# Attention of a seven-layer kernel: from head by head to units of four heads by 512 queries

## The chip, the core and the metric

The kernel runs on one core of a Trainium2 chip. The time is the device's, in microseconds (us), from one execution to the next of the whole program; less is better. The engines are PE (TensorE, with its weight loads PEld), DVE (VectorE), ACT (ScalarE), POOL (GpSimd) and SP (SyncE, which here only issues DMAs).

## The reference

One sequence of 2048 tokens of 128 channels passes through a chain of layers, each added to x: softmax attention with 16 heads of 8 channels (rotary positions, RMS norm of q and k), a small spline feed-forward, retention, the feed-forward again, linear attention, then twice a layer with a convolution, softmax attention and a mixture of four experts, with an RWKV layer between the two. Softmax attention so stands three times in the program, and is all that the change touches:

```python
attn = jnp.einsum('bqhd,bkhd->bhqk', q, k) * scale
attn = jnp.where(causal[None, None], attn, -jnp.inf)
attn = jax.nn.softmax(attn, axis=-1)
out = jnp.einsum('bhqk,bkhd->bqhd', attn, v).reshape(B, T, C)
```

All in float32, with B = 1, T = 2048, C = 128, 16 heads, D = 8.

## The kernel before

`qkv_stage` (L424) projects q, k and v, splits q and k into three bf16 parts each (so that nine products of parts give float32 precision) and stores them, turned, in DRAM as `q_parts` and `k_parts`. After a barrier `attention_stage` (L682) begins, and after it `output_stage` turns and projects the result.

Attention goes head by head. For a head SP loads 72 rows (3 x 3 parts x 8 channels) of q and of k, 2048 columns each, twice: into `q_max`/`k_max` for the maxima and into `q_exp`/`k_exp` for the scores (`load_rows`, L768, L769; six DMAs of 96 KB for each pair of buffers). All four have two slots, for even and odd heads.

The pass over maxima (`max_unit`, PE L902, DVE L1021) puts queries on partitions: a product of 128 queries by up to 512 keys, on the diagonal a second product that adds the mask (L905), and a reduction on DVE, through a ring of three PSUM banks `stat`. A head has 41 such reductions. When a group of query tiles is complete DVE makes its maximum, split into a high and a low bf16 (`row_max`, L1030 to L1032); PE turns these (`shift_unit`, L911), DVE copies them out (L1039), and SP writes them as two more rows below the 72 of `q_exp` (`load_shift`, L797), against rows of -1 in `k_exp`. So the second product gives the score minus its row's maximum. There are three such groups per head.

The second pass puts keys on partitions. A unit is two key tiles by 512 queries, 1024 columns (less on the diagonal); a head has 20 (`EXPU`). PE makes the scores (L924) into one of two double banks, ACT takes the exponential into one of four slots of `probs` (L884), POOL zeroes the triangle on the diagonal (L854), and PE multiplies with the values (`pv`, L934). The values of a head, with a column of ones for the denominator, are 32 columns of weights; the four query tiles of 128 columns go to the four strips of 32 columns of the array, so that eight products of 128 columns serve a unit. They accumulate in one bank for the whole head, which ACT copies out (L873), PE turns (L915) and DVE divides (L1045, L1046).

The order on PE is written out by hand: for each unit e it waits for exponential e, issues the scores of e + 2, the values of e, and the entries of `PLAN` for e, which are the maxima of the next head, spread evenly (two a unit), and at fixed places the shift rows and the output of the head before. The first head's 41 maxima come ahead of everything (`FIRST_PLAN`), and the last head runs without maxima. PE and DVE walk the ring in the same order. Heads 1 to 14 are a loop over pairs of heads on every engine. POOL gathers the values of the next head (L833).

SP's order is, for each head: the loads of maxima for head h + 2, those of scores for h + 1, then the shift rows.

Of the kernel before, what the change touches and what calls it, by code (L numbers as in the profile page):

```python
# [89 lines left out]
def load_stage(k, d, w):  # L90

    nc = k.nc
    with ExitStack() as ctx:
# [15 lines left out]
        with nc.Block() as block:  # L109
# [22 lines left out]
            @block.vector  # L132
            def _(dve):
                for n, name in enumerate(("q_max", "q_exp")):
                    nc.vector.memset(w[name][64:P, :, :], 0.0).then_inc(padded[0].sem, 1)
                dve.wait_ge(loaded.sem, loaded.at(16 * len(plain)))
                nc.vector.tensor_copy(w["mask16"][:], maskf[:]).then_inc(kept.sem, 1)
                nc.vector.tensor_copy(w["ident16"][:], w["ident"][:]).then_inc(kept.sem, 1)

            @block.gpsimd  # L140
            def _(pool):
                for n, name in enumerate(("k_max", "k_exp")):
                    nc.gpsimd.memset(w[name][64:P, :, :], -1.0).then_inc(padded[1].sem, 1)
                    pool.wait_ge(padded[1].sem, padded[1].at(n + 1))

        loaded.done(16 * len(plain))
        for sig in padded:
            sig.done(2)
# [532 lines left out]

def attention_stage(k, w, v, parts_dram, scale, y):  # L682

    nc = k.nc
    MAXU = []
    for i in range(NT):
        pieces = [(c * BANK, min(BANK, (i + 1) * P - c * BANK)) for c in range(i // QC + 1)]
        if i == NT - 1:
            pieces[0:1] = [(0, BANK // 2), (BANK // 2, BANK // 2)]
        MAXU += [(i, at, width, n) for n, (at, width) in enumerate(pieces)]
    EXPU = []  # L700
    for j in range(NQ):
        for u in range(2 * j):
            EXPU.append((j, [(2 * u, 0), (2 * u + 1, 0)]))
        EXPU.append((j, [(QC * j, 0), (QC * j + 1, 1)]))
        EXPU.append((j, [(QC * j + 2, 2), (QC * j + 3, 3)]))
    NM, NE = len(MAXU), len(EXPU)

    OWN = [e for e in range(NE) if EXPU[e][1][0][0] >= QC * EXPU[e][0]]
    VT = NT // len(OWN)
    VN = len(OWN) - 1  # L710
    GROUPS = [(0, 2), (2, 3), (3, 4)]
    NG = len(GROUPS)
    MAX_END = [sum(i < QC * hi for i, *_ in MAXU) for _, hi in GROUPS]
    FIRST_EXP = [min(e for e in range(NE) if EXPU[e][0] == lo) for lo, _ in GROUPS]


    OWN_AT, NEXT_AT, OUT_AT = 2, (9, 15), 0
    PLAN = []
    for e in range(NE):
        if e == OWN_AT:  # L720
            PLAN.append((e, "own_shift", NG - 1))
        for g, at in enumerate(NEXT_AT):
            if e == at:
                PLAN.append((e, "next_shift", g))
        PLAN += [(e, "max", u) for u in range(e * NM // NE, (e + 1) * NM // NE)]
        if e == OUT_AT:
            PLAN.append((e, "out", None))
    HEAD0_PLAN = [p for p in PLAN if p[1] != "out"]
    LAST_PLAN = [p for p in PLAN if p[1] in ("own_shift", "out")] + [(NE, "own_out", None)]
    FIRST_PLAN = [(0, "max", u) for u in range(NM)] + [(0, "next_shift", g) for g in range(NG - 1)]  # L730
    STATU, PRE = len(PLAN), len(FIRST_PLAN)
    AT, AT0 = ({(kind, arg): n for n, (_, kind, arg) in enumerate(plan)} for plan in (PLAN, HEAD0_PLAN))
    for g, at in enumerate(NEXT_AT):
        assert AT["max", MAX_END[g] - 1] < AT["next_shift", g]
    RING, PSLOTS = 3, 4
    assert STATU % RING == 0 and NE % PSLOTS == 0 and NE % 2 == 0
    TAIL = PRE - 1 + (H - 1) * STATU
    counts = []
    with ExitStack() as ctx:
        qm, km, qe, ke = w["q_max"], w["k_max"], w["q_exp"], w["k_exp"]  # L740
        probs = k.sb("probs", [P, PSLOTS, 2 * BANK], F32, ctx)
        vh = k.sb("v_head", [P, 2, NT, 32], F32, ctx)
        early = k.sb("v_early", [P, 2 * VT, D], F32, ctx)
        mpart = k.sb("max_part", [P, 2, NT, NQ + 1], F32, ctx)
        mx = k.sb("row_max", [P, 2, NT], F32, ctx)
        mxb = k.sb("row_max_parts", [P, 2, SHIFT * NT], BF16, ctx)
        mxt = [k.sb(f"row_max_turned{g}", [SHIFT * QC * (hi - lo), 2, P], BF16, ctx) for g, (lo, hi) in enumerate(GROUPS)]
        ot = k.sb("out_turned", [P, 2, BANK], F32, ctx)
        rden = k.sb("inv_denominator", [P, 2, NT], F32, ctx)
        ring = [k.ps(f"stat{n}", [P, BANK], ctx) for n in range(RING)]  # L750
        sc = [k.ps(f"score{n}", [P, 2 * BANK], ctx) for n in range(2)]
        acc = k.ps("pv", [P, BANK], ctx)

        m_loaded = [k.counter(f"max_rows_loaded{n}") for n in range(2)]
        e_loaded = [k.counter(f"exp_rows_loaded{n}") for n in range(2)]
        shift_in = [[k.counter(f"shift_rows_loaded{n}_{g}") for g in range(NG)] for n in range(2)]
# [3 lines left out]
        out_copied, v_ready, cut = k.counter("pv_copied_out"), k.counter("v_head_ready"), k.counter("probs_masked")  # L760
        v_early = k.counter("v_early_rows")
        q_rows, k_rows = (parts_dram[s].rearrange("a (h d) t -> h a d t", d=D) for s in range(2))

        def load_rows(sp, qt, kt, par, h, loaded):

            for a in range(PARTS):
                at = slice(a * PARTS * D, (a + 1) * PARTS * D)
                sp.dma_start(qt[at, par, :], bcast(q_rows[h, a], 0, PARTS)).then_inc(loaded.sem, 16)  # L768
                sp.dma_start(kt[at, par, :], k_rows[h]).then_inc(loaded.sem, 16)  # L769

        NL = 2 * PARTS * 16
        NS = SHIFT * 16

        def base(h):

            return PRE if isinstance(h, int) and h == 0 else h * STATU + (PRE - 1)

        with nc.Block() as block:


            @block.sync
            def _(sp):
                def load_max(h, par):
                    load_rows(sp, qm, km, par, h, m_loaded[par])

                def load_exp(h, par, prev):
                    if prev is not None:
                        sp.wait_ge(scored.sem, scored.at(NE * prev + NE))
                    load_rows(sp, qe, ke, par, h, e_loaded[par])

                def load_shift(par, g, used):
                    sp.wait_ge(stat_used.sem, stat_used.at(used))
                    lo, hi = GROUPS[g]
                    nt = QC * (hi - lo)
                    for n in range(SHIFT):
                        r = KROWS + n
                        sp.dma_start(qe[r:r + 1, par, lo * BANK:hi * BANK].rearrange("o (i q) -> o i q", q=P),  # L797
                                     mxt[g][n * nt:(n + 1) * nt, par, :]).then_inc(shift_in[par][g].sem, 16)
# [4 lines left out]
                for g in range(NG - 1):  # L803
                    load_shift(0, g, NM + g + 1)
# [1429 lines left out]
```

## Time and profile before

| what | time |
|---|---|
| median of three runs | 3068.51 us |
| lowest and highest | 3059.32 and 3070.42 us |
| span of the profiled execution | 3064.6 us |
| PE busy | 2459.5 us (80%) |
| DVE busy | 1968.9 us (64%) |
| ACT busy | 1467.3 us (48%) |
| POOL busy | 542.6 us (18%) |

The profile gives no time of its own for the profiled execution beside its span; the median of the runs is 3.9 us above the span. Busy times are sums over the whole program. As PE is pipelined and the ends of its products are modelled, its busy share is no measure of how near it is to its peak: distances between starts say more. The clock that the chip grants PE is at one of two levels, 1.2 or 2.4 GHz; in a stretch the profile gives the mean as a share of the higher.

### The profile page before, as it was taken

Reading aid. Unit: us, or ns where it says so; the run is one execution under the profiler, and the core shown is the slowest. Engines: PE = TensorE matmul, PEld = TensorE weight load, DVE = VectorE, ACT = ScalarE, POOL = GpSimd, SP = SyncE. Lnnn points to the kernel's source line nnn. Section 1 sums busy time; section 2 is a strip of 40 time slices with the busy share of each in tenths; the row PEclk is TensorE's granted clock in tenths of the full one; section 3 lists DMA queues with packets and bytes.
Section 4 is the critical chain, followed back from the end, with each engine's and each line's share of the span. In section 5 each row is a group of like instructions: output and inputs, shape, how many; then the busy total and the mean of one; then the engine's idle time right before and its main releaser. Section 6 shows DMA issues by size and latency. Waiting matters only on the chain. (4 is left out here: it accounts for less than half of the span.)

```text
span 3064.6 us, 68154 instructions
## 1 busy us (share of the span) xinstructions
PE 2459.5 (80%) x23684; PEld 1331.0 (43%) x23684; DVE 1968.9 (64%) x4246; ACT 1467.3 (48%) x2102; POOL 542.6 (18%) x1023
## 2 busy tenths in 40 slices
PE   3698998994699538648998999897138899999898
PEld 2244444453344325424444444565123444444565
DVE  6576676757477774567777776334957677777333
ACT  3254455564599545334555555323233555555422
POOL 4011111111244315140111111000340111111100
PEclk7699999996799768869999999999668999999899
DMA  3101110000111000010010000000011000010000
GB/s 105 71 33 37 38 38 34 33 10 0 57 48 49 12 0 1 0 65 32 33 40 36 31 31 24 1 0 0 0 50 44 35 31 31 38 40 23 1 1 14
DMA packets 45622, 89.65 MB, mean 29 GB/s; under 512 B 9104, under 2 KB 27792, under 8 KB 45456
## 3 DMA queue, kind: packets, MB, share of 16 engines
q1 hardware_dynamic: 45456, 87.34, 7.8%
q8 instruction: 116, 1.90, 0.3%
q14 instruction: 50, 0.41, 0.0%
HBM read 73.29 MB, written 13.63 MB: 28 GB/s over the span
## 5 line engine op out<-in xcount | busy, mean ns | idle before, releaser
L1021 DVE TENSOR_REDUCE max_part<-stat 128x1 f32<-128x512 f32 (+3 forms) x1968 | 1074.9, 595 | 407.8 <-PE stat L902 203.0
L884 ACT ACTIVATE probs<-score 128x1024 f32<-128x1024 f32 (+1 forms) x960 | 859.5, 896 | 807.0 <-PE score L924 804.7
L934 PE MATMUL pv<-probs,v_head 128*32 128x128 f32 x13056 | 635.4, 285 | 0.5 <-POOL probs L854 0.5
L924 PE MATMUL score<-q_exp,k_exp 128*128 128x512 bf16 (+3 forms) x1920 | 536.5, 363 | 121.0 <-DMA q_exp<-row_max_turned 100.0
L902 PE MATMUL stat<-k_max,q_max 128*128 128x512 bf16 (+3 forms) x1968 | 581.7, 365 | 64.0 <-DMA k_max<-k_parts 48.4
L934 PEld LDWEIGHTS pv<-probs,v_head 128*32 128x32 f32 x13056 | 367.7, 111 | 301.7 <-issue 279.8
L902 PEld LDWEIGHTS stat<-k_max,q_max 128*128 128x128 bf16 x1968 | 162.0, 100 | 324.2 <-DVE max_part L1021 131.5
L833 POOL COPY v_head<-qkv 128x16 f32 (+2 forms) x258 | 51.1, 199 | 1191.1 <-ACT probs L884 1190.4
L924 PEld LDWEIGHTS score<-q_exp,k_exp 128*128 128x128 bf16 x1920 | 140.9, 98 | 276.3 <-issue 209.4
L1978 ACT ACTIVATE gate<-gate_ps 128x512 f32<-128x512 f32 x128 | 76.4, 597 | 264.0 <-PE gate_ps L1953 264.0
L854 POOL TENSOR_SCALAR_AFFINE_SELECT probs<-probs 128x256 f32<-128x256 f32 x384 | 155.9, 406 | 251.4 <-ACT probs L884 251.2
L1652 ACT ACTIVATE abs_act_ps<-abs_act_ps 128x1024 f32<-128x1024 f32 (+3 forms) x176 | 167.5, 952 | 27.4 <-PE abs_act_ps L1607 27.3
L905 PE MATMUL stat<-mask,ident 128*128 128x128 bf16 x768 | 174.9, 230 | 0.0
L2018 DVE TENSOR_TENSOR hidden<-value_ps,gate 128x512 f32<-128x512 f32 x128 | 88.6, 692 | 112.1 <-PE value_ps L1954 112.0
L1684 DVE TENSOR_REDUCE abs_part<-abs_dve_ps 128x512 f32 (+5 forms) x224 | 108.5, 515 | 44.4 <-PE abs_dve_ps L1621 43.2
L1953 PE MATMUL gate_ps<-ln_t,expert_wv 128*128 (+1 forms) x256 | 133.2, 602 | 0.0
L1954 PE MATMUL value_ps<-ln_t,expert_wv 128*128 (+1 forms) x256 | 132.5, 599 | 0.0
L1943 PEld LDWEIGHTS expert_ps<-expert_proj,hidden 128*128 128x128 f32 x1024 | 119.2, 192 | 17.7 <-issue 17.7
L1943 PE MATMUL expert_ps<-expert_proj,hidden 128*128 128x128 f32 x1024 | 119.6, 275 | 1.8 <-DVE hidden L2018 1.8
L905 PEld LDWEIGHTS stat<-mask,ident 128*128 128x128 bf16 x768 | 79.7, 104 | 65.8 <-issue 12.5
L1607 PE MATMUL abs_act_ps<-k_max,q_max 128*128 128x512 bf16 x352 | 100.0, 371 | 7.0 <-ACT abs_act_ps L1652 4.2
L2007 DVE SCALAR_TENSOR_TENSOR X<-expert_ps,pick,X 128x128 f32 (+1 forms) x128 | 37.5, 346 | 98.2 <-PE expert_ps L1943 98.2
(268 smaller groups left out, 2569.8 us busy)
## 6 DMA issues: line engine op xcount, KB each, us to landing
q_max<-q_parts SPq DMA_DIRECT2D x192, 96.0 KB
k_max<-k_parts SPq DMA_DIRECT2D x192, 96.0 KB
q_exp<-q_parts SPq DMA_DIRECT2D x144, 96.0 KB
k_exp<-k_parts SPq DMA_DIRECT2D x144, 96.0 KB
q_parts<-parts_t SPq DMA_DIRECT2D x16, 384.0 KB, 2.6
k_parts<-parts_t SPq DMA_DIRECT2D x16, 384.0 KB, 3.3
q_exp<-row_max_turned SPq DMA_DIRECT2D x192, 1.0 KB
expert_wv<-in_L_ffn_expert_wv SPq DMA_DIRECT2D x1, 2048.0 KB, 8.5
```

Of the source, the lines that this page charges most:

```text
L854: nc.gpsimd.affine_select(tile, tile, [[0, 2], [1, P]], ALU.is_ge, 0.0, base=0, channel_multiplier=-1).then_inc(cut.sem, 1)
L884: nc.scalar.activation(probs[:, e % PSLOTS, 0:width], sc[e % 2][:, 0:width], ACT.Exp, scale=scale).then_inc(expd.sem, 1)
L902: last = nc.tensor.matmul(out[:, 0:width], qm[:, par, i * P:(i + 1) * P], km[:, par, at:at + width], start=True, stop=not own)
L905: last = nc.tensor.matmul(out[:, width - P:width], w["ident16"][:], w["mask16"][:], start=False, stop=True)
L924: last = nc.tensor.matmul(out, ke[:, par, kt * P:(kt + 1) * P], qe[:, par, j * BANK + f * P:(j + 1) * BANK], start=True, stop=True)
L934: last = nc.tensor.matmul(acc[32 * c:32 * c + 32, j * P:(j + 1) * P], vh[:, par, kt, :], probs[:, e % PSLOTS, at:at + P], start=kt == 0, s ...
L1021: nc.vector.reduce_max(mpart[:, par, i, col:col + 1], ring[at % RING][:, 0:width], AX.X).then_inc(stat_used.sem, 1)
L1652: nc.scalar.activation(ps, ps, ACT.Abs, accum_out=part[:, bass.ds(h, 1), i, 0:1]).then_inc(a_used.sem, 1)
L1684: nc.vector.tensor_reduce(part[:, bass.ds(h, 1), i, slot:slot + 1], d_ps[n % DRING][:, 0:width], AX.X, ALU.add, apply_absolute_value=True) ...
L1943: ins = nc.tensor.matmul(op[e % 2][:, s * P:(s + 1) * P], hid[:, e % 2, f, s * P:(s + 1) * P], w["expert_proj"][:, e % E, f, :], start=f = ...
L1953: nc.tensor.matmul(gp[g % 2][:], w["expert_wv"][:, e, f * P:(f + 1) * P], rhs, start=True, stop=True).then_inc(upped.sem, 1)
L1954: nc.tensor.matmul(vp[g % 2][:], w["expert_wv"][:, e, DFF + f * P:DFF + (f + 1) * P], rhs, start=True, stop=True).then_inc(upped.sem, 1)
```

## The change

A unit is now four heads by 512 queries, against all keys up to them: 16 units, in the order `UNITS` (group of heads, block j of queries), each of 4(j + 1) steps of one key tile, 160 steps in all. A step has two score products of 512 columns for each half of the heads, one exponential for each half, and four value products of 512 columns, one per head, each with nine columns of weights (8 channels and the ones) in a strip of its own. `attention_plan` makes the order of the ring: maxima of later units, spread so that each unit's are complete some three steps before its first step, shift rows once per unit (after the first three maxima of the next one), outputs three steps after a unit's end. The ring has 640 maxima, 16 shift rows and 16 outputs. Both passes share one set of rows, in three buffers (`uq`, `uk`); a unit's rows come by 24 DMAs, twelve of 24 KB for the queries and twelve of 24(j + 1) KB for the keys, and the rows of -1 by 12 DMAs at the start. The values are copied once into `v9`. Everything is unrolled, with no loop. `probs` has six slots of half a step. `q_exp` and `k_exp` are gone from the weights, with their memsets in `load_stage`, and `qkv_stage` is called ahead of `softmax_layer`, whose result goes over q's place in `qkv`. The core of the diff, where "..." stands for what is left out:

```diff
+HG = 4
+NG = H // HG
+BUFS = 3
+UNITS = [(0, 0), (0, 1), (0, 2), (0, 3), (1, 3), (2, 3), (3, 3), (1, 2), (2, 2), (3, 2), (1, 1), (1, 0), (2, 1), (2, 0), (3, 1), (3, 0)]
+def attention_plan():
+    steps = [(u, kt) for u, (_, j) in enumerate(UNITS) for kt in range(QC * (j + 1))]
+    first = [min(t for t, (v, _) in enumerate(steps) if v == u) for u in range(len(UNITS))]
+    last = [max(t for t, (v, _) in enumerate(steps) if v == u) for u in range(len(UNITS))]
+    stream, due = [], []
+    for u, (_, j) in enumerate(UNITS):
+        maxima = [("max", u, (h, s, c)) for s in range(QC) for c in range(j + 1) for h in range(HG)]
+        stream += maxima[:LATE] if u else maxima
+        if u:
+            stream.append(("shift", u - 1, None))
+            stream += maxima[LATE:]
+        due.append((len(stream) + LATE + 1, max(1, first[u] - 3) if u else 0))
+    stream.append(("shift", len(UNITS) - 1, None))
+    free = [min(first[u - BUFS + 1] + 3, first[u - 1] - 2) if u >= BUFS else -1 for u in range(len(UNITS))]
+    ring, at = [], 0
+    for t in range(-1, len(steps)):
+        for half in range(2):
+            for u in range(len(UNITS)):
+                if t == last[u] + 3 and half == 1:
+                    ring.append((t, half, "out", u, None))
+            if t < 0:
+                want = due[0][0] if half else 0
+            else:
+                room = [(min(n, len(stream)) - at, 2 * (d - t) - half) for n, d in due]
+                want = at + max([0] + [-(-n // max(1, left)) for n, left in room if n > 0])
+            while at < min(want, len(stream)) and t >= free[stream[at][1]]:
+                ring.append((t, half) + stream[at])
+                at += 1
...
+LATE = 3
...
+                def load(u):
+                    g, j = UNITS[u]
+                    b = u % BUFS
+                    if u >= BUFS:
+                        sp.wait_ge(scored.sem, scored.at(2 * LAST[u - BUFS] + 2))
+                    keys = BANK * (j + 1)
+                    for h in range(HG):
+                        for a in range(PARTS):
+                            at = slice(a * PARTS * D, (a + 1) * PARTS * D)
+                            sp.dma_start(uk[at, b, h, 0:keys], k_rows[g * HG + h][:, :, 0:keys]).then_inc(loaded[b].sem, 16)
+                            sp.dma_start(uq[at, b, h, :], bcast(q_rows[g * HG + h, a][:, j * BANK:(j + 1) * BANK], 0, PARTS)).then_inc(loaded[b].sem, 16)
...
+                load(0)
+                sp.wait_ge(minus_ready.sem, minus_ready.at(1))
+                for b in range(BUFS):
+                    for h in range(HG):
+                        sp.dma_start(uk[KROWS:ROWS, b, h, :].rearrange("r (c t) -> r c t", t=BANK), bcast(minus[:], 1, NQ)).then_inc(minus_loaded.sem, 16)
+                load(1)
+                load(2)
+                load_shift(0)
+                for u in range(NU):
+                    if u + 1 < NU:
+                        load_shift(u + 1)
+                    if u + BUFS < NU:
+                        load(u + BUFS)
...
+                        if kind == "max" and arg == (0, 0, 0):
+                            pe.wait_ge(loaded[u % BUFS].sem, loaded[u % BUFS].at(loads_of(u)))
+                        elif kind == "shift":
+                            pe.wait_ge(max_ready.sem, max_ready.at(u + 1))
+                        elif kind == "out":
+                            pe.wait_ge(out_copied.sem, out_copied.at(u + 1))
...
+                def pv(t):
...
+                    for h in range(HG):
+                        last = nc.tensor.matmul(acc[32 * h:32 * h + D + 1, f:BANK], v9[:, kt, g * HG + h, :], probs[:, (2 * t + h // 2) % PSLOTS, h % 2, 0:BANK - f],
+                                                start=kt == 0, stop=kt == QC * j + QC - 1, tile_position=(0, 32 * h))
...
+                for t in range(NS):
+                    pe.wait_ge(expd.sem, expd.at(2 * t + 1))
+                    if t + 1 < NS:
+                        scores(t + 1, 0)
+                    fill_ring(t, 0)
+                    if t > 0:
+                        pv(t - 1)
+                    pe.wait_ge(expd.sem, expd.at(2 * t + 2))
+                    if t + 1 < NS:
+                        scores(t + 1, 1)
+                    fill_ring(t, 1)
...
-                for n, name in enumerate(("k_max", "k_exp")):
-                    nc.gpsimd.memset(w[name][64:P, :, :], -1.0).then_inc(padded[1].sem, 1)
+                nc.gpsimd.memset(w["k_max"][64:P, :, :], -1.0).then_inc(padded[1].sem, 1)
```

## Rows read from the trace of the kernel before

**Rows 1.** Stretches, first to last exponential of each stage: length, each engine's busy time, granted clock, DMA.

```profile
127.30:674.90 547.60, 499.19 (x5932) 247.12 (x5929) 376.14 (x826) 294.87 (x335) 69.27 (x253) 0.94 0.09 34
1391.30:1926.10 534.80, 496.27 (x5931) 244.18 (x5929) 375.27 (x826) 294.52 (x335) 68.60 (x253) 0.95 0.09 33
2325.30:2858.90 533.60, 494.14 (x5931) 243.66 (x5929) 375.33 (x826) 294.55 (x335) 68.59 (x253) 0.96 0.09 33
```

**Rows 2.** Instructions of line 884 by stage: ns min/median/max, first and last start.

```profile
L884 ACT ACTIVATE probs<-score x320: 484/1024/1026, 127.3 to 674.4; 128x1024 f32<-128x1024 f32 x96, 128x896 f32<-128x896 f32 x64
L884 ACT ACTIVATE probs<-score x320: 484/1024/1026, 1391.3 to 1925.6; 128x1024 f32<-128x1024 f32 x96, 128x896 f32<-128x896 f32 x64
L884 ACT ACTIVATE probs<-score x320: 484/1024/1026, 2325.3 to 2858.4; 128x1024 f32<-128x1024 f32 x96, 128x896 f32<-128x896 f32 x64
```

**Rows 3.** Waits, 1400 to 1900 us: in total, times, longest.

```profile
PE score L924 <- DMA q_exp<-row_max_turned: 34.8, 14, 3.2
```

**Rows 4.** Timeline, second stage: a unit of a head with maxima (start, length, engine).

```profile
1434.34 0.61 PE L924 MATMUL score<-q_exp,k_exp 128*128 128x512 bf16 x2
...
1434.88 0.65 PE L934 MATMUL pv<-probs,v_head 128*32 128x128 f32 x16
...
1435.46 0.60 PE L902 MATMUL stat<-k_max,q_max 128*128 128x512 bf16 x2
...
1435.90 0.59 PE L924 MATMUL score<-q_exp,k_exp 128*128 128x512 bf16 x2
```

**Rows 5.** Timeline, second stage: units of the last head, without maxima.

```profile
1921.94 0.60 PE L924 MATMUL score<-q_exp,k_exp 128*128 128x512 bf16 x2
...
1922.48 0.64 PE L934 MATMUL pv<-probs,v_head 128*32 128x128 f32 x16
...
1923.06 0.61 PE L924 MATMUL score<-q_exp,k_exp 128*128 128x512 bf16 x2
```

**Rows 6.** Stretches of 0.02 us, value products alone: PE records under way in brackets.

```profile
311.36:311.38 0.02, 0.02 (x4) 0.02 (x4) 0.00 (x0) 1.00 0.53 205
...
311.48:311.50 0.02, 0.02 (x6) 0.02 (x7) 0.00 (x0) 1.00 0.00 0
```

**Rows 7.** Groups by line: busy us, mean ns, idle before; experts' gate products and value products.

```profile
L1953 PE MATMUL gate_ps<-ln_t,expert_wv 128*128 (+1 forms) x256 | 133.2, 602 | 0.0
L934 PE MATMUL pv<-probs,v_head 128*32 128x128 f32 x4332 | 210.3, 285 | 0.0
```

**Rows 8.** Timeline, start of the first attention stage.

```profile
89.51 0.91 SPq L768 DMA_DIRECT2D q_max<-q_parts  x1
...
98.72 0.70 SPq L768 DMA_DIRECT2D q_exp<-q_parts  x1
99.46 0.70 SPq L769 DMA_DIRECT2D k_exp<-k_parts  x1
...
100.71 5.89 DVE L1021 TENSOR_REDUCE max_part<-stat 128x1 f32<-128x128 f32 x12 [10.90 <-PE stat L905]
...
123.81 2.65 SPq L797 DMA_DIRECT2D q_exp<-row_max_turned  x4
...
126.40 1.23 PE L924 MATMUL score<-q_exp,k_exp 128*128 128x512 bf16 x4 [3.58 <-DMA q_exp<-row_max_turned]
```

**Rows 9.** Stretches of 1 us, stores and loads; last two columns: DMA share of 16 engines, GB/s.

```profile
87.00:88.00 1.00, 0.00 (x0) 0.00 (x0) 0.00 (x0) 0.00 (x0) 0.00 (x0) 0.50 0.99 355
97.00:98.00 1.00, 0.00 (x0) 0.00 (x0) 0.00 (x0) 0.00 (x0) 0.00 (x0) 0.50 0.18 74
```

**Rows 10.** SP's instructions by line, whole program: ns min/median/max; shift rows, then stores.

```profile
L797 SPq DMA_DIRECT2D q_exp<-row_max_turned x288: 572/614/742, 123.8 to 2844.2; - x144
L655 SPq DMA_DIRECT2D q_parts<-parts_t x16: 372/372/407, 64.1 to 2283.1; - x16
L655 SPq DMA_DIRECT2D k_parts<-parts_t x16: 477/489/1402, 64.6 to 2283.6; - x16
```

More of the change, by code:

```diff
@@ L676, in qkv_stage @@
                 sig.done(NQ)
+HG = 4
[30 more added lines that the diff above has]
+                at += 1
+    for u in range(len(UNITS)):
+        if last[u] + 3 >= len(steps):
+            ring.append((len(steps), 1, "out", u, None))
+    assert at == len(stream)
+    return steps, first, last, ring
@@ L706, in attention_stage @@
[L706 to L734, printed above, removed]
@@ L918, in scores @@
-                def scores(e, par):
-                    j, tiles = EXPU[e]
-                    at = 0
-                    for kt, f in tiles:
-                        width = BANK - f * P
-                        out = sc[e % 2][:, at:at + width]
-                        last = nc.tensor.matmul(out, ke[:, par, kt * P:(kt + 1) * P],
-                                                qe[:, par, j * BANK + f * P:(j + 1) * BANK], start=True, stop=True)
-                        at += width
-                    last.then_inc(scored.sem, 1)
@@ new lines, in scores @@
+                def scores(t, hp):
+                    u, kt = STEPS[t]
+                    b, f = u % BUFS, first_col(t)
+                    if hp == 0 and t == FIRST[u]:
+                        pe.wait_ge(shift_in.sem, shift_in.at(SHIFT * 16 * (u + 1)))
+                    for i in range(2):
+                        h = 2 * hp + i
+                        last = nc.tensor.matmul(sc[hp][:, i, 0:BANK - f], uk[0:ROWS, b, h, kt * P:(kt + 1) * P], uq[0:ROWS, b, h, f:BANK],
+                                                start=True, stop=True)
+                    last.then_inc(scored.sem, 1)
@@ L1073, in _ @@
-                body(0, None, 0, plan=HEAD0_PLAN)
-                before = steps[1]
-                body(1, None, 1)
-                per_head = steps[1] - before
-                before = steps[1]
-                with dve.Fori(1, H // 2 - 1) as i:
-                    for par in range(2):
-                        steps[0], steps[1] = i * (2 * per_head) + (before - 2 * per_head), par * per_head
-                        body(2 * i + par, i, par)
-                steps[0], steps[1] = before + (H - 4) * per_head, 0
```

476 lines of the change are left out of this document (175 added, 301 removed).

## The prediction

> **What bounds the kernel now.** I began with the stretches between the first and the last exponential of the three attention stages [rows 1]. They last 547.6, 534.8 and 533.6 us, over half of the span of 3064.6 us. PE is busy for 91 to 93% of each, DVE 69 to 70%, ACT 54 to 55%, POOL 13%, and the clock granted is 0.94 to 0.96, nearly all at the 2.4 GHz level. So PE's order of work sets the pace there, and I looked for what PE spends beside streaming. The first and last times of the exponentials [rows 2] with the timeline of a stage's start [rows 8] give what lies ahead: from SP's first load at 89.5 to the first exponential at 127.3, 37.8 us; the other stages issue the same loads in the same order, and I take the same. The waits of one stage [rows 3] show PE's only large one: 34.8 us in 14 waits for a head's shift rows. Two pieces of the timeline give the step. With maxima, scores begin at 1434.34, value products at 1434.88, maxima at 1435.46, the next scores at 1435.90: 1.56 us [rows 4]. In the last head, without maxima, scores begin every 1.12 us (1921.94, 1923.06) [rows 5]. An exponential of 1024 columns takes 1.02 us [rows 2].
>
> **What the step is made of.** Two maxima cost PE 0.44 us, 0.22 per 512 columns of bf16 [rows 4], so two score products stream 0.43 too. The 16 records of the value product start four at a time, about 0.11 to 0.12 us apart [rows 6], so they stream some 0.43. The step of 1.12 thus holds 0.86 of streaming and 0.26 of changing over: scores to values takes 0.54 for 0.43, values to the next 0.58 for 0.43 [rows 4, 5].
>
> **The value products.** The same columns stream: four heads by 512 columns in four column strips instead of four query tiles of one head. A record of 512 fp32 columns lasts 602 ns and one of 128 columns 285 [rows 7]: 384 more columns cost 0.32, so 512 stream 0.43, and the two records of a product 0.85, the streaming of two old units. What falls away is one change-over in two: 0.26 for each of 160 steps. A full step without ring work costs PE 2 x 0.43 + 0.85 + 0.26 = 1.97, below ACT's 2 x 1.02 + gaps = 2.15. With four ring entries it is 1.97 + 0.88 + about 0.05 for masks = 2.9, where before two units took 3.12. Exponentials keep their number, 320, and their columns.
>
> That four strips stream abreast is seen here at 128 columns [rows 6]; at 512 columns nothing here shows it, and I take it over from there. A page speaks against this: in the Trainium skill (TensorE: Matmul & The Clock Gate, Part 3, the table of measured speedups) packing four tiles of 512 columns gained 3.07 times, not four. By that figure the step's 0.85 would be 1.11, an estimate from the page; the rows at 128 columns do not agree with it.
>
> **Start of a stage, +28 us.** Ahead of the first shift rows SP will issue 24 loads for unit 0, 12 for the -1 rows, and 24 each for units 1 and 2: 84, where it issued 18. Issues of this pattern begin 0.74 apart [rows 8]. Landing does not bind: three of the sixteen engines carry them (share 0.18) at 74 GB/s [rows 9], and the new ones carry 24 to 96 KB, mostly in rows of 1 to 3 KB. Stores in rows of 1 KB moved 355 GB/s at a share of 0.99, 22 per engine [rows 9]; three engines do 66, so 24 KB takes 0.37. Only a pair of 96 + 24 KB (j = 3) needs 120/74 = 1.62 against 1.48, some 19.5 a load. Then 84 x 0.743 = 62.4; from the shift issue to the scores 2.59, to the exponential 0.94 [rows 2, 8]: 65.9 against 37.8. Unit 0 needs only 16 maxima where head 0 needed 41, but they wait for nothing that ends last any more. Clearing the accumulator, the ones and the copy of v (POOL, ACT, DVE) lie under these 66 us; with that cover gone the copy of 2048 columns would cost about 2 us.
>
> **The body.** The plan written in the diff, counted out: step 0 gets 33 ring entries, steps 1 to 18 six each, 19 to 112 four, and in the last 47 steps 13 get six to eight, 5 four, 8 two or three, 21 none or one. DVE back to back took 5.89 us for 12 reductions of 384 columns on average, 0.49 each [rows 8].
> - Step 0: 33 x 0.53 = 17.5 (a mean of 406 columns, and the small operations).
> - Steps 1 to 18: 448 columns, 6 x 0.56 = 3.4; 61.
> - Steps 19 to 112: 94 x 2.9 = 273, less 10: in 28 diagonal steps the shorter scores and values gain until DVE's 4 x 0.6 = 2.4 binds; 263.
> - The last 47: 13 x 3.3 + 5 x 2.9 + 8 x 2.3 + 10 x 2.15 + 11 x 1.5 (diagonal) = 114.
> - 16 turned outputs at 0.8 and 16 ends of maxima, when the ring waits for three small operations, at 0.6: 23.
>
> Together 478. Then the wait that the change adds. SP may load unit u+3 only when unit u has all its scores; 24 issues take 17.8 us and the last lands some 1.9 later, 19.7. PE waits for it at that unit's first maximum, and scores, values and shift rows of the earlier units are queued behind it. The plan sets what lies between. For unit 12 the load may begin half way in step 122 and the maximum stands in step 127: half a step 0.7, a diagonal one 1.2, three without ring work at 2.25, together 8.7, so PE lacks 11. In the same way unit 11 (steps 110 to 115, 11.0 us) lacks 9, unit 13 (130 to 134, 8.9) 11, unit 14 (134 to 139, 14.4, its load held up 2 by shift rows) 7, unit 15 (142 to 146, 8.8) 11, units 9 and 10 (6 steps, 16.5) 3 each, unit 3 2: 57, and 3 more for shift rows behind a load on SP. That is 60, in the place of 34.8 of shift waits. Sum 538, against 547.6, 534.8 and 533.6: -10, +3, +4. Out of the loop's registers the code runs unrolled; I cost fetching it at nothing, since PE needs fewer instructions than before per step.
>
> The memsets that load_stage loses lie under its input loads, and the move of qkv_stage out of softmax_layer only changes lifetimes: nothing.
>
> **Sum.** 3 x 28 - 3 = +81 to +82: 3064.6 + 82 = 3146.6 for the span. The median of the runs, 3068.5, is 3.9 above the profiled span: **3150 us**, 2.7% slower.
>
> Bounds. An issue costs between 0.47 (0.37 and 0.49 of the stores, with the gap of 0.04) and 0.95 (0.91 of a stage's first load) [rows 8, 10]. I take 0.74, from the same pattern. The late waits lie between 0 and 90 us a stage, the full step between 2.7 and 3.1 (+-19 us a stage).
>
> **Rivals.**
> A, not slower: with their short rows the new loads issue faster. Shift rows, of 256 bytes, issue in 0.57 to 0.74, median 0.61 [rows 10], 0.65 with the gap: the start gains 8, seven late waits 2.2 each, 23 a stage, giving 3081. At 0.47 the start gains 23, the waits 41: 2958. It decides from about 0.61 per issue down. For: the size of the rows is all that changes. Against: the stores have rows of 1 KB too, and there every issue moves four times the bytes of a load for 0.4, so size does not seem to set it; the pattern (24 rows on three engines) stays. 0.19.
> B, the late waits hardly appear, because steps there run longer than I put them or a unit's loads land sooner: minus 57 x 3, 2979. Against: SP's issues alone fill 17.8. 0.07.
> C, one strip in four runs alone at 512 columns: 0.85 x 4/3 = 1.14, 0.28 more on 136 full steps' worth, 39 a stage: 3266. For: nothing of that width here. Against: all four abreast at 128 [rows 6]. 0.09. It is the case of the page named above.
> D, the strips don't run abreast at nine columns of weights: 3 x 0.85 x 136 more a stage, near 4190. 0.02.
> E, a row of 1 KB costs an engine as much as one of 4 KB: 1.28 per load; start +45, waits +100 a stage: near 3590. Against: the stores [rows 9]. 0.02.
> The forecast has 0.61, its own range 3085 to 3215.
>
> **How the numbers follow.** About 0.5% is what a measurement tells from no change (3053 to 3084). Faster: the lower half of A, B, a little of the forecast's tail, 0.17. Same: the rest of A and some tail, 0.14. Slower: 0.69. The range reaches into A and B below and to C above and leaves out the rest: 3030 to 3260.
>
> **What would show it.** The first exponential 66 us after SP's first load; SP's issues 0.74 apart; PE waiting for unit loads at the first maximum of units 11 to 15, 7 to 11 us each; a full step of 2.9 with four entries; values of 0.85 + 0.2 as a group of eight records; the wait for shift rows down to some us. If the steps with four entries take over 3.1, the packing step is wrong; if the start takes under 55, the issue price is; if the stage's last third shows no waits for loads, the plan's slack was misread. All three low at once would make it faster than before.

## The result, and the profile after

The changed kernel takes **3179.1 us** (median of 4 runs, 3176.3 to 3187.3), the kernel before 3069.5 in the same session (4 runs): a ratio of 1.037, 95% interval 1.034 to 1.039. I had predicted 3150, 2.7% slower; it is 3.7% slower. The run profiled took 3187.3 with a span of 3185.6, which is 121.0 more than before's 3064.6. It is the slowest of the four, 8 us above their median, so that the accounts below, which go by its profile, hold that much more than the medians do.

From the page of the kernel after: span, busy times, and four groups of the attention stages.

```profile
span 3185.6 us, 41521 instructions
PE 2347.6 (74%) x14293; PEld 1042.1 (33%) x14324; DVE 1873.6 (59%) x3816; ACT 1435.5 (45%) x2105; POOL 486.3 (15%) x635
L944 DVE TENSOR_REDUCE max_part<-stat 128x1 f32<-128x512 f32 (+3 forms) x1920 | 1044.8, 604 | 610.5 <-PE stat L851 339.2
L851 PE MATMUL stat<-unit_k,unit_q 72*128 72x512 bf16 (+3 forms) x1920 | 632.0, 386 | 360.7 <-DMA unit_q<-q_parts 320.5
L892 PE MATMUL score<-unit_q,unit_k 74*128 74x512 bf16 (+3 forms) x1920 | 541.8, 369 | 55.6 <-DMA unit_q<-row_max_turned 50.5
L905 PE MATMUL pv<-probs,v_ones 128*9 128x512 f32 (+3 forms) x3840 | 477.2, 570 | 1.6 <-ACT out_turned L828 0.7
```

No engine is fuller than before. What is new stands in the idle columns: TensorE's maxima (L851) waited 320.5 us for the rows of a unit, 138 of them at the three starts and 183 late in the stages.

Stretches from the first to the last exponential of the three stages (to hold against [rows 1]); below them the second stage cut at the starts of steps 19 and 113.

```profile
153.20:705.30 552.10, 472.92 (x2847) 151.93 (x2844) 356.67 (x710) 282.15 (x335) 51.24 (x128) 0.88 0.08 26
1445.60:1998.70 553.10, 474.91 (x2842) 152.44 (x2843) 356.38 (x709) 282.42 (x335) 51.03 (x127) 0.88 0.08 26
2427.50:2978.60 551.10, 472.24 (x2842) 151.49 (x2844) 356.30 (x709) 282.13 (x335) 51.03 (x127) 0.88 0.08 26
...
1538.00:1817.70 279.70, 267.43 (x1644) 85.50 (x1643) 216.59 (x413) 169.27 (x195) 22.42 (x56) 0.96 0.08 28
1817.70:1998.70 181.00, 122.05 (x800) 40.82 (x801) 65.28 (x153) 78.28 (x102) 22.11 (x55) 0.80 0.07 20
```

TensorE is busy 21 to 26 us less in a stage than before, yet the stretches are 4.5, 18.3 and 17.5 us longer, and the granted clock fell from 0.94 to 0.96 to 0.88.

The start of the second stage, SP's queue and the first scores and exponential (compare [rows 8]):

```profile
1378.92 0.79 SPq L782 DMA_DIRECT2D unit_k<-k_parts  x1
1379.76 0.73 SPq L783 DMA_DIRECT2D unit_q<-q_parts  x1
...
1441.14 1.21 SPq L791 DMA_DIRECT2D unit_q<-row_max_turned  x2
...
1444.57 1.86 PE L892 MATMUL score<-unit_q,unit_k 74*128 74x512 bf16 x4 [17.14 <-DMA unit_q<-row_max_turned]
...
1445.62 2.82 ACT L837 ACTIVATE probs<-score 128x1024 f32<-128x1024 f32 x3 [61.44 <-PE score L892]
```

The loads are issued 0.74 us apart, the shift rows follow 62.2 us after the first load, the first exponential after 66.7 (66.2 and 66.6 in the other stages), where the stage before took 37.8. Three starts of +28.7 are +86, three bodies +40; the rest of the program is 5 shorter: 121.

A full step with four maxima in the same stage (timeline, from the scores of one to those of the next), and TensorE's waits for a unit's rows late in the stage:

```profile
1648.11 1.04 PE L905 MATMUL pv<-probs,v_ones 128*9 128x512 f32 x8
1649.09 0.60 PE L892 MATMUL score<-unit_q,unit_k 74*128 74x512 bf16 x2
...
1651.02 1.04 PE L905 MATMUL pv<-probs,v_ones 128*9 128x512 f32 x8
1651.99 0.61 PE L892 MATMUL score<-unit_q,unit_k 74*128 74x512 bf16 x2
```

```profile
1753.18 1.04 PE L851 MATMUL stat<-unit_k,unit_q 72*128 72x512 bf16 x2 [3.73 <-DMA unit_q<-q_parts]
1794.03 0.61 PE L851 MATMUL stat<-unit_k,unit_q 72*128 72x512 bf16 x1 [2.67 <-DMA unit_q<-q_parts]
1834.07 0.29 PE L851 MATMUL stat<-unit_k,unit_q 72*128 72x128 bf16 x1 [9.72 <-DMA unit_q<-q_parts]
1876.18 1.46 PE L851 MATMUL stat<-unit_k,unit_q 72*128 72x512 bf16 x3 [12.22 <-DMA unit_q<-q_parts]
1912.67 0.29 PE L851 MATMUL stat<-unit_k,unit_q 72*128 72x128 bf16 x1 [11.89 <-DMA unit_q<-q_parts]
1935.78 1.46 PE L851 MATMUL stat<-unit_k,unit_q 72*128 72x512 bf16 x3 [8.17 <-DMA unit_q<-q_parts]
1970.55 0.29 PE L851 MATMUL stat<-unit_k,unit_q 72*128 72x128 bf16 x1 [11.90 <-DMA unit_q<-q_parts]
```

The step lasts 2.90 us, and the values of four heads lead to the next scores after 0.97 to 0.98: the eight products would stream 3.4 us one after another at 0.43 each, so four strips run abreast at 512 columns too. The seven waits are those of units 9 to 15, 60.3 us (61.6 and 60.9 in the other stages); unit 3 has none.

### The profile page after: what moved, and what is told of

It reads as the page before. It is cut to its first block and busy times, and to the rows that moved or that the text cites. A ratio compares the mean times of both kernels' runs of the same rounds, so it can differ in the third digit from the quotient of the medians.

```text
span 3185.6 us, 41521 instructions
## 1 busy us (share of the span) xinstructions
PE 2347.6 (74%) x14293; PEld 1042.1 (33%) x14324; DVE 1873.6 (59%) x3816; ACT 1435.5 (45%) x2105; POOL 486.3 (15%) x635
## 5 line engine op out<-in xcount | busy, mean ns | idle before, releaser
L944 DVE TENSOR_REDUCE max_part<-stat 128x1 f32<-128x512 f32 (+3 forms) x1920 | 1044.8, 604 | 610.5 <-PE stat L851 339.2
L837 ACT ACTIVATE probs<-score 128x1024 f32<-128x1024 f32 x960 | 828.4, 896 | 984.1 <-PE score L892 979.5
L851 PE MATMUL stat<-unit_k,unit_q 72*128 72x512 bf16 (+3 forms) x1920 | 632.0, 386 | 360.7 <-DMA unit_q<-q_parts 320.5
L892 PE MATMUL score<-unit_q,unit_k 74*128 74x512 bf16 (+3 forms) x1920 | 541.8, 369 | 55.6 <-DMA unit_q<-row_max_turned 50.5
L905 PE MATMUL pv<-probs,v_ones 128*9 128x512 f32 (+3 forms) x3840 | 477.2, 570 | 1.6 <-ACT out_turned L828 0.7
L851 PEld LDWEIGHTS stat<-unit_k,unit_q 72*128 72x128 bf16 x1920 | 196.2, 103 | 683.8 <-DMA unit_q<-q_parts 331.0
L892 PEld LDWEIGHTS score<-unit_q,unit_k 74*128 74x128 bf16 x1920 | 142.7, 100 | 524.6 <-ACT probs L837 246.6
L1498 PE MATMUL abs_act_ps<-k_max,q_max 128*128 128x512 bf16 (+1 forms) x321 | 93.6, 371 | 12.9 <-ACT abs_act_ps L1543 8.8
L905 PEld LDWEIGHTS pv<-probs,v_ones 128*9 128x9 f32 x3840 | 58.9, 89 | 124.3 <-issue 103.9
L967 DVE RECIPROCAL inv_denominator<-stat 128x16 f32<-128x16 f32 x48 | 12.4, 258 | 125.9 <-PE stat L863 125.9
```

What stands on the lines that cost most here:

```text
L837: nc.scalar.activation(probs[:, n % PSLOTS, :, 0:width], sc[hp][:, :, 0:width], ACT.Exp, scale=scale).then_inc(expd.sem, 1)
L851: last = nc.tensor.matmul(out[:, 0:width], uq[0:KROWS, b, h, s * P:(s + 1) * P], uk[0:KROWS, b, h, c * BANK:c * BANK + width], start=True, ...
L892: last = nc.tensor.matmul(sc[hp][:, i, 0:BANK - f], uk[0:ROWS, b, h, kt * P:(kt + 1) * P], uq[0:ROWS, b, h, f:BANK], start=True, stop=True)
L905: last = nc.tensor.matmul(acc[32 * h:32 * h + D + 1, f:BANK], v9[:, kt, g * HG + h, :], probs[:, (2 * t + h // 2) % PSLOTS, h % 2, 0:BANK ...
L944: nc.vector.reduce_max(mpart[:, u % 2, col, c:c + 1], ring[n % RBANKS][:, 0:width], AX.X).then_inc(stat_used.sem, 1)
```

## The experiments

The theory to be tested: the time lost is issue time on SP's queue, at the start of a stage and again when a short unit frees its buffer; a part of the body that the prediction did not have hangs on TensorE's clock. The rivals: the landing of small DMAs, VectorE's pace, and the change-over between full-array products and strips.

### Units 9 to 15 load nothing

```
 def load(u):
...
+    if u >= KEEP:      # 9
+        return
```

> Units 9 to 15 load no rows of keys and queries (they compute on what lies in the buffer; their shift rows are still loaded). Left out: 7 x 24 of the 384 load DMAs of a stage. If late loads are what the first maxima of units 9 to 15 wait for, as SP issues 24 DMAs in 17.8 us after the unit three before it has ended: the 60.3 us of these waits in a stage go, and the stage body falls from 552 to about 492-498 us, the program from 3179 to about 3000 (-180). If the time only moves (VectorE or the exponentials bound the short units, or the plan's maxima then wait elsewhere), less than half of it comes back: over 3090. The start of the stages (66 us) and the four-entry step (2.9 us) stay as they are in either case.

Measured: **2959.5 us** (2 runs, 0.966 of before, interval 0.963 to 0.969) with units 9 to 15 computing on old rows, 219.6 less than with the loads, 40 more than the waits account for. The first three lines are steps 0 to 18 of the three stages, the last two the second stage's steps 19 to 112 and 113 to the end:

```profile
154.80:241.50 86.70, 77.89 (x401) 24.07 (x399) 74.16 (x145) 34.69 (x41) 6.50 (x16) 0.86 0.10 35
1363.80:1456.10 92.30, 85.34 (x402) 26.12 (x399) 74.37 (x145) 34.71 (x40) 6.50 (x16) 0.76 0.09 33
2267.40:2365.10 97.70, 91.41 (x402) 27.55 (x399) 74.72 (x145) 34.74 (x40) 6.50 (x16) 0.70 0.09 31
...
1456.10:1720.00 263.90, 257.81 (x1643) 84.10 (x1643) 215.80 (x412) 168.80 (x194) 22.42 (x56) 1.00 0.06 21
1720.00:1836.30 116.30, 107.92 (x797) 37.23 (x794) 65.09 (x154) 78.02 (x102) 22.09 (x55) 1.00 0.01 1
```

Two things follow. With the waits, the clock's falls behind them go as well. The same 800 products of the last 47 steps keep TensorE busy for 107.9 us at a clock of 1.00, and for 122.1 at 0.80 in the changed kernel; steps 19 to 112 for 257.8 at 1.00 against 267.4 at 0.96. In the changed kernel's trace the clock falls to 1.2 GHz in the course of each longer late wait and stays there for 4 to 10 us after the wait has ended: 72 of the second stage's last 181 us, 32 of them behind the waits. From step 19 on a stage takes 457.8 us with the late loads (mean of three) and 380.2 without: they cost 77.6, of which 61 is waiting and 17 what comes after it. That is by the profiled runs; the medians are 73 a stage apart.

And the first 19 steps, the same work in every stage, take 86.7, 92.3 or 97.7 us as the clock is 0.86, 0.76 or 0.70: 25, 45 and 59 us at 1.2 GHz, 0.32 us lost for each. Drawn out to none of it, the line ends at 79. It is an extrapolation; no stage of this order ran without such a stretch.

### Value products in two halves of the columns

```
-    acc[.., f:BANK]          <- probs[.., 0:BANK - f]
+    acc[.., f + lo:f + hi]   <- probs[.., lo:hi]      # part 0 behind the first half step, part 1 behind the second
```

> The value products of a step are issued in two halves of the columns, one behind each half step, as before the change (144 of 160 steps; the first of each unit stays whole). Same columns, same strips, only one more change between full-array matmuls and strips in a step and twice the instructions. If a change-over costs the 0.26 us that I took for it: +37 us in a stage body, +112 us in all, 3290. If the price of it was hidden by the pipeline of TensorE or is paid by VectorE's slack: under +30 us in all.

Measured: **3265.7 us** (2 runs, ratio 1.066, interval 1.060 to 1.072), 86.5 more than undivided. A full step, scores to scores of the next step, from its timeline:

```profile
1650.94 0.60 PE L892 MATMUL score<-unit_q,unit_k 74*128 74x512 bf16 x2
...
1653.98 0.60 PE L892 MATMUL score<-unit_q,unit_k 74*128 74x512 bf16 x2
```

3.04 us against 2.90: a step is 0.14 longer. That is less than the price of the second visit to the strips, because something else goes at the same time. In the undivided step the four maxima come in a bunch, and TensorE's weight loads wait for VectorE to free a bank of the ring (18.0 us of such waits in 154 us, 1566 to 1720); here they come two by two, and the wait is gone (0.7 us in 160, 1600 to 1760). The undivided step without that hold stands in the run with half reductions below:

```profile
1404.88 0.61 PE L896 MATMUL score<-unit_q,unit_k 74*128 74x512 bf16 x2
...
1407.69 0.61 PE L896 MATMUL score<-unit_q,unit_k 74*128 74x512 bf16 x2
```

2.81 us. So a second visit costs 0.23, and VectorE's hold on the ring 0.09 in each full step of the changed kernel. The 0.14 times 144 steps and three stages is 60 us. The remaining 26 I put down to longer stretches at 1.2 GHz: steps 19 to 112 of its second stage take 318.8 us at a clock of 0.85. In one stretch of it the clock stays down although TensorE is nearly full (113 us at 0.50, TensorE busy for 111.5 of them; it began with a late wait of 2.2 us):

```profile
1794.00:1907.00 113.00, 111.49 (x559) 29.34 (x560) 47.92 (x92) 40.76 (x47) 6.53 (x16) 0.50 0.05 14
```

### TensorE kept busy ahead of the first scores

```
+ turn_over(60)      # 128x128 fp32 products into a free bank, ahead of unit 0's rows
  fill_ring(-1, 1)   # 70 more ahead of unit 1's first maximum
+ turn_over(60)      # ahead of the first scores
```

> 190 products of 128 x 128 fp32 identities fill TensorE's three waits at the start of each attention stage (60 ahead of unit 0's rows, 70 ahead of unit 1's, 60 ahead of the shift rows; results unused). If the granted clock of 0.50 to 0.75 in the first 70 us of a stage's steps follows from TensorE idling for 60 us ahead of them: the clock of that stretch rises to 0.9 or more, steps 0 to 18 fall from 92-96 us to 79-83, and the program gets 25 to 45 us shorter (about 3140), even if the filling itself takes up to 3 us more than the waits. If the lower clock comes with the stretch whatever went before it (the load of the steps themselves): the time stays, 3175 to 3195.

Measured: **3171.6 us** (4 runs, ratio 1.036, interval 1.032 to 1.039): 7.5 less, within what two such medians differ by. The stretch before the first exponential of the second stage, then the first 24 us of its steps, then the rest up to step 19:

```profile
1435.00:1445.00 10.00, 9.11 (x82) 8.91 (x80) 0.00 (x0) 0.00 (x0) 0.00 (x0) 1.00 0.19 63
1445.90:1469.70 23.80, 21.61 (x72) 6.02 (x71) 19.55 (x40) 4.16 (x5) 2.04 (x5) 0.52 0.01 1
1469.70:1532.80 63.10, 55.71 (x331) 18.01 (x328) 54.58 (x105) 30.51 (x35) 4.49 (x11) 0.99 0.13 48
```

The filling did lift the clock to 1.00, but 0.7 us after the first exponential (1.3 and 1.9 us in the other stages) it fell to 1.2 GHz again, for 24 us here and for 41 and 51 in the other stages. Without filling it was 45, 54 and 53; but the kernel without late loads, whose starts idle as long as the changed kernel's, has 25, 45 and 59. So filling has no effect that stands out of this spread, and my theory of the slow stretch fails. These steps are the densest in maxima, and VectorE is busy for 19.6 of the 23.8 us, yet its hold on TensorE is not what brings the clock down. TensorE's products around the fall, with its waits:

```profile
1445.31 1.02 PE L898 MATMUL score<-unit_q,unit_k 74*128 74x512 bf16 x4 [1.20 <-DMA unit_q<-row_max_turned]
1447.10 0.80 PE L898 MATMUL score<-unit_q,unit_k 74*128 74x384 bf16 x2 [0.77 <-ACT probs L837]
...
1449.12 0.29 PE L851 MATMUL stat<-unit_k,unit_q 72*128 72x128 bf16 x1 [0.36 <-DVE max_part L952]
```

The clock was 1.00 up to 1446.5 and 0.50 from 1446.8, while TensorE waited 0.77 us for the first exponential; its first wait for VectorE came 2 us later. In the other two stages, too, the clock fell before that wait began.

### All four heads in one DMA

The parts are stored head by head, so that the 24 rows of a slot lie at one stride; the keys keep their order in each slot and the queries' parts are rotated against them, which covers the same nine pairs.

```
- for h in range(HG): for a in range(PARTS):   # 24 DMAs
-     sp.dma_start(uk[at, b, h, 0:keys], k_rows[g * HG + h][:, :, 0:keys])
-     sp.dma_start(uq[at, b, h, :], bcast(q_rows[g * HG + h, a][...], 0, PARTS))
+ for a in range(PARTS):                       # 8 DMAs
+     sp.dma_start(uk[at, b, :, 0:keys], k_rows[heads, ...] as "(a d) h t")
+     sp.dma_start(uq[.., b, :, :], q_rows[heads, lo:hi, ...] as "(a d) h t")   # lo:hi = a:3, 0:a
```

> The parts lie in memory head by head (head, part, channel), so that one DMA loads 24 rows of all four heads: 3 DMAs of keys and 5 of queries in a unit in place of 24, same bytes; in return each store of parts is three DMAs. If the issue of 0.74 us on SP is what a unit's load costs: 8 issues take 5.9 us in place of 17.8; the start of a stage falls by 2 x 11.9 us at least (unit 0 and unit 1 to the first exponential: 66.5 to about 31-43), and the late waits of 60 us in a stage nearly vanish (each is under 12.3 us). Sum -75 to -95 us in a stage, 2895 to 2955. If instead what counts is the landing (a DMA of 24 rows moved 74 GB/s here, and a unit of the longest kind has 1.47 MB, 20 us at that rate): the first units gain little and the late waits stay within a third of what they are, 3100 or more.

Measured: **2847.3 us** (4 runs, ratio 0.929, interval 0.927 to 0.930): 332 less than the changed kernel and 7.1% faster than the kernel before. The start takes 29.5 to 29.8 us, the body 474.8 to 476.2. The 10 us that end 2 us ahead of the second stage's first exponential, and its steps by the same cuts as above:

```profile
1290.00:1300.00 10.00, 1.73 (x4) 0.39 (x4) 2.00 (x4) 0.00 (x0) 0.00 (x0) 0.50 0.71 126
...
1301.90:1397.50 95.60, 89.17 (x401) 26.84 (x399) 74.65 (x145) 34.77 (x40) 6.54 (x16) 0.72 0.16 32
1397.50:1661.50 264.00, 257.92 (x1644) 84.13 (x1643) 215.92 (x413) 168.94 (x195) 22.52 (x56) 1.00 0.16 31
1661.50:1778.10 116.60, 108.02 (x800) 37.25 (x802) 64.99 (x153) 77.99 (x102) 22.21 (x55) 1.00 0.14 28
```

From step 19 on it is the kernel without late loads, to 0.5 us, with every row loaded. It beats my own figure (2895 to 2955) for two reasons: the clock behind the waits, and the price of an issue, which I had left at 0.74 and which is 0.31. SP's instructions by line, ns min/median/max, in this kernel and then in the changed one:

```profile
L783 SPq DMA_DIRECT2D unit_k<-k_parts x144: 298/305/1637, 89.2 to 2614.7; - x144
```

```profile
L782 SPq DMA_DIRECT2D unit_k<-k_parts x576: 699/700/920, 87.0 to 2947.5; - x192
```

### The same rows, one head in a DMA

```
  for h in range(HG): for a in range(PARTS):   # 12 DMAs of keys, 20 of queries
      sp.dma_start(uk[at, b, h, 0:keys], k_rows[g * HG + h, ...] as "(a d) t")
...
```

> heads_in_one (2847 us), with each head in a DMA of its own again: 12 DMAs of keys and 20 of queries in a unit, where the change has 12 and 12. What is new against the change is only that the rows of a DMA lie at one stride in memory. The merged DMAs took SP 0.30 to 0.38 us each, the change's 0.70. If that fall comes from the single stride: 32 issues take 12 us in place of the change's 17.8; the start falls by 17 us and the late waits by 35 to 45 us in a stage against the change: 2980 to 3020. If each issue of 24 rows of one head still takes 0.7 us, a unit takes 23 us: 3280 to 3330.

Measured: **3002.5 us** (2 runs, ratio 0.980, interval 0.977 to 0.982). Its loads on SP by line, and the second stage's start:

```profile
L783 SPq DMA_DIRECT2D unit_k<-k_parts x576: 297/364/1974, 88.6 to 2767.3; - x192
...
1322.26 0.32 SPq L783 DMA_DIRECT2D unit_k<-k_parts  x1
...
1370.53 1.94 ACT L841 ACTIVATE probs<-score 128x1024 f32<-128x1024 f32 x2 [43.01 <-PE score L896]
```

The same 24 rows of the same length take half the time to issue once the 24 lie at one stride instead of three groups of eight. With a third more DMAs than the changed kernel, this one takes 177 us less. Of the 332 us that the merged loads gave, the stride alone so gives over half; the four heads in one DMA give the other 155.

### The start with a second queue

```
+ act.dma_start(uq[at, u, h, :], ...)    # the 36 query loads of units 0 to 2, on ScalarE's queue
```

> The kernel after the change, with the 36 DMAs of queries of units 0, 1 and 2 issued by ScalarE, beside the 36 of keys on SP; same DMAs, same bytes, late units as they are. If it is one queue's issue of 0.74 us that sets the start: SP's part of 62.4 us falls to 35.6, first exponential 39 to 42 us after the first load in place of 66.5, -75 us in all, 3095 to 3110. If the landing of the small DMAs sets it, the start stays over 55 us: 3150 or more.

Measured: **3115.1 us** (2 runs, ratio 1.016, interval 1.014 to 1.019), 64 less. The second stage's start:

```profile
1347.00 9.07 SPq L782 DMA_DIRECT2D unit_k<-k_parts  x12
1347.01 26.66 ACTq L825 DMA_DIRECT2D unit_q<-q_parts  x36
...
1382.98 1.21 SPq L792 DMA_DIRECT2D unit_q<-row_max_turned  x2
...
1392.26 1.86 PE L899 MATMUL score<-unit_q,unit_k 74*128 74x512 bf16 x4 [10.25 <-DMA unit_q<-row_max_turned]
```

```profile
1384.00:1392.00 8.00, 0.00 (x0) 0.00 (x0) 0.00 (x0) 0.00 (x0) 0.00 (x0) 0.50 0.18 69
```

Both queues issue at 0.74 to 0.76, side by side, and the shift rows leave after 36.0 us, as expected. Then they take 9 us to land, behind loads that drain at 69 GB/s over 0.18 of the DMA engines. So issue bound the start, and with two queues the landing is the next bound: 46.3 us instead of the 39 to 42 expected.

### Shift rows ahead of unit 2's loads

```
  load(1)
+ load_shift(0)
  load(2)
- load_shift(0)
```

> The kernel after the change (3179 us), unit 0's shift rows sent ahead of unit 2's 24 loads. If the order of issue on SP sets the first exponential: it comes 51 to 53 us after the first load in place of 66.5, -40 to -45 us in all, 3130 to 3145. If the rows of unit 1's maxima (which the ring puts ahead of the shift's transpose) set it: no more than 5 us in a stage, 3160 or more.

Measured: **3141.0 us** (2 runs, ratio 1.025, interval 1.021 to 1.030), 38 less; the first exponential of the second stage comes 52.9 us after the first load (1366.34 to 1419.19). Time and start lie where the order of issue on SP was to put them.

### Both, with the minus rows in one DMA

```
  load(0)
- for b in range(BUFS): for h in range(HG): sp.dma_start(uk[KROWS:ROWS, b, h, :], ...)   # 12
+ sp.dma_start(uk[KROWS:ROWS] as "r (b h c) t", bcast(minus, 1, BUFS * HG * NQ))         # 1
  load(1)
+ load_shift(0)
  load(2)
- load_shift(0)
```

> heads_in_one (2847 us), with the 12 DMAs of the rows of minus one as a single DMA, and with unit 0's shift rows sent ahead of unit 2's loads. In heads_in_one a stage's first exponential comes 30 us after its first load. If SP's issues still set the start, 11 issues of 0.7 us and the 8 ahead of the shift rows go: -8 to -11 us in a stage, 2815 to 2823. If the landing sets it (up to 143 GB/s and 0.81 of the DMA engines' time were seen in that stretch): putting unit 2's bytes behind the shift rows gives some of it, the minus rows nothing: -3 to -6 us in a stage, 2829 to 2838. Body 475 us in either case.

Measured: **2828.0 us** (4 runs, ratio 0.924, interval 0.921 to 0.926): the fastest, 19 less than the merged loads alone. Starts of 23.6, 22.4 and 22.6 us, 6 to 7 less each. That lies between the two bands, -8 to -11 for issues and -3 to -6 for landing; I read it as neither setting the start alone once a unit has 8 DMAs, but no run here takes the two apart.

### VectorE reduces half of each bank

```
- nc.vector.reduce_max(.., ring[n % RBANKS][:, 0:width], ..)
+ nc.vector.reduce_max(.., ring[n % RBANKS][:, 0:min(width, BANK // 2)], ..)
```

> heads_in_one (2847 us), with VectorE reducing only the first 256 columns of each bank of maxima: left out are the other columns of the row maxima. VectorE's 683 ns for 512 columns fall to about 350. If TensorE bounds the steps 19 to 112 (busy 176 of 180 us, VectorE 148): they keep 264 us but for 5 at most; 2825 to 2850. If VectorE does (its ring holds TensorE up, four reductions are 2.73 of a step's 2.81 us): these steps fall by 20 us or more in a stage, under 2790.

Measured: **2741.2 us** (2 runs, ratio 0.894, interval 0.891 to 0.897), 106 less than the merged loads alone. Second stage, steps 0 to 18 and 19 to 112:

```profile
1261.40:1333.90 72.50, 70.81 (x401) 25.62 (x399) 50.15 (x146) 34.61 (x40) 6.53 (x16) 0.85 0.22 42
1333.90:1584.80 250.90, 250.76 (x1644) 84.71 (x1643) 142.87 (x412) 168.68 (x195) 22.53 (x56) 1.00 0.17 32
```

Neither reading was right. Steps 19 to 112 lose 13 us, between the two figures, and TensorE is then busy without a gap: it paces them, with the 5% that VectorE's hold on the ring adds. VectorE is not full (216 of the 264 us); it holds TensorE because the maxima come in bunches. The surprise is ahead: steps 0 to 18 fall from 95.6 to 72.5 us, and their time at 1.2 GHz from 53 to 22 us in each stage.

### The units in another order

```
- UNITS = [(0, 0), (0, 1), (0, 2), (0, 3), (1, 3), ...]
+ UNITS = [(0, 0), (1, 0), (0, 1), (3, 1), (0, 2), (2, 2), (0, 3), (1, 1), (3, 3), (2, 1), (1, 3), ...]
```

> one_and_shift_first (2828 us) with the units in another order: two short units first, and short ones between the long ones, so that the maxima of the next unit are spread more evenly (in the order of the change, steps 0 to 18 hold about 145 of a stage's 640 maxima, 7 or 8 in a step, and halving VectorE's reductions shortened these steps by 22 us in a stage, the 94 behind them by 13). If VectorE's pace in the dense steps is what stretches the start: the body of a stage falls by about 10 us, from 473 to about 463, the program to 2790-2805. If the sum of TensorE's work sets the body wherever the maxima lie: within 10 us of 2828. Over 2840 if the next unit's rows now come late between short units.

Measured: **2832.1 us** (4 runs, ratio 0.926, interval 0.921 to 0.930), no difference from 2828.0. The starts are 3 us shorter (19.2 to 20.3), as the second unit is a short one, and the bodies 2 us longer on average. The first 19 steps, which hold fewer maxima in this order, take 6 us less (85.6 on average against 91.7, where the stages of the other order alone range from 85.7 to 97.7), those behind them 8 more. Spreading the maxima moved them and saved nothing; that TensorE's products, the same in number, set the body is the reading that fits.

## Why the prediction was right

- **Start of a stage, +28.** Right to 1 us: 84 issues of 0.743, 65.9 us, measured 66.2 to 66.7. Two queues bring it to 46, where landing binds. Rival A was wrong for this kernel (0.70 an issue, as the pattern said), but its idea was sound: there is a cheaper issue, and it takes another arrangement of the rows, not shorter ones.
- **The full step, 2.9.** Measured 2.90. That it fits so well is in part luck: without masks my sum was 2.85, and nothing in it stood for VectorE's hold of 0.09; the same step without the hold takes 2.81. Value products of 0.85 with a change-over: 0.98 to the next scores. This rules out C and D. The Trainium skill (TensorE: Matmul & The Clock Gate, Part 3, the table of measured speedups) gives its gain of 3.07 for four tiles of rows, not of columns as here. The trace does not agree with that figure for this form: eight records of 512 fp32 columns and nine weights pass in 0.98 us, nearly four abreast. E falls too: a kilobyte row was no dearer.
- **The change-over, 0.26.** Near: the divided products put one back for 0.23 (3.04 against 2.81, both without VectorE's hold). 2.81 less the streaming of 2.58 (three times 0.86) leaves the same 0.23 for the one that stays.
- **Late waits, 57 and 3.** The waits for rows are right, which rules out B, nearly one by one: 3.7, 2.7, 9.7, 12.2, 11.9, 8.2, 11.9 for units 9 to 15 where I had 3, 3, 9, 11, 11, 7, 11; unit 3's 2 and the 3 for shift rows did not come. What they cost is 77.6, since the clock falls behind each.
- **The body without them, 478.** Measured 475, by two errors that cancel: luck. Steps 19 to 112: 263 predicted, 264.0, of which 13 are VectorE's hold, that I did not have. The last 47: 114, and 116. Steps 0 to 18: 78.5 predicted, 92 to 96 measured. The 23 us for turned outputs and ends of maxima: nothing is left for them once these three are added up (264 + 116 + 95 = 475), so I take them to have been inside the steps as I priced them.

The step that failed is a **term left out**: TensorE's clock. I priced every step from rows at a clock near 1.00 and never asked what the new waits and the dense first steps do to it, although the clock rows of before stood beside the stretches [rows 1]. Against the 538 of the sum a body takes 552: +16 in steps 0 to 18, +18 for the late waits, +3 in the rest, -23 for the outputs. Three such bodies are +42, three starts +2, what lies outside -5: the 39 us by which the span's 3146.6 was missed. (The medians miss by 29: 3179.1 against 3150. The profiled run is 8 us above its median, and its span only 1.7 us below its time where I took 3.9.) What made the rest of the program 5 us shorter no run shows.

Open remains what brings the clock down in the first steps and what keeps it there. Filling the idle time ahead of them shows no clear effect (41, 24 and 51 us at 1.2 GHz, against 25 to 59 in kernels without filling). Half reductions shorten it (22 us in every stage, against 53 with whole ones), so VectorE's work plays some part in how long it stays down, but with TensorE filled the clock fell before TensorE had waited for VectorE at all. Nor was a version tried whose first steps run at full clock throughout, so the 79 us stay extrapolated.

## What to carry to other kernels

When a loop over heads becomes a loop over larger units, count the DMA issues of each unit on its queue, and hold them against the shortest time in which a unit's buffer comes free: here 24 issues of 0.74 us stood against 9 to 16 us of work, and the issues, at the start and late in the stage, made the difference between 3.7% slower and 7.6% faster than before. Before giving up such a change, look at the shape of each transfer: rows at one stride in memory, and several heads in one DMA, took a unit's load from 17.8 to about 3 us of queue time. Price a new wait at more than its length where TensorE's clock falls behind it; here 17 of the 78 us that late loads cost a stage were slower work after the waits.

## What the runs showed of the hardware that I had not expected

- The time of an issue on SP depends on the layout of the rows. 24 rows in three groups of eight: 0.70 us, whether a broadcast makes the groups (queries) or a stride does (keys). 24 rows at one stride: 0.36 for one head, 0.31 for four heads at once. Why, no run shows.
- Rows at one stride move faster as well: 126 GB/s over 10 us at 0.71 of the engines with four heads in a DMA, and 115 to 131 GB/s at 0.38 to 0.51 with one (head by head, 1400 to 1410 us), where loads in three groups of eight ran at 69 and 74 GB/s at 0.18 [rows 9].
- The clock can stay at 1.2 GHz through 113 us of which TensorE is busy for 111.5, and can fall to it less than 2 us after a stretch of 10 us at full clock and 91% busy, with a wait of 1.20 us between and in a second one of 0.77.
- After each of the 21 late waits of the changed kernel, 2.7 to 12.2 us long, the clock was at 1.2 GHz for another 4 to 10 us.
